# Column statistics from transposed messages, nodes in two parts, and an opening with its row tables shared out anew

## The reference, cut to what matters

```python
h = concatenate([x[dst], x[src], edge_attr], axis=1)            # x here is layernorm(x)
gate = sigmoid(_bn(silu(h @ W1f + b1f) @ W2f + b2f, g_int, beta_int))
msg = gate * (silu(h @ W1m + b1m) @ W2m + b2m)
agg = segment_sum(msg, dst, num_segments=N)
x = x + relu(xln + _bn(agg, g_bn, beta_bn))                     # _bn: mean and variance over the rows of each column
xn = layernorm(x)
gate_logits = xn @ Wg + bg + bias;  top-2 of 8, softmax -> combine
h = relu(einsum('td,edh->teh', xn, W1) + b1)
y = einsum('teh,ehd->ted', h, W2) + b2
x = x + einsum('ted,te->td', y, combine)
```

## Time and profile before

| | |
|---|---|
| median of three executions | 841.52 us |
| the profiled execution | 839.38 us |
| its span | 837.3 us |
| TensorE busy | 783.9 us (94%) |
| VectorE / ScalarE / GpSimd busy | 518.7 / 451.9 / 454.9 us |
| mean granted clock of TensorE | 0.965 of 2.4 GHz |

### The profile page before, as it was taken

One profiled execution on the slowest core, in us unless ns is written; L12 is line 12 of the kernel. 1 busy time (PEld: TensorE's weight loads), 2 busy tenths in 40 slices (PEclk: granted clock), 3 DMA queues, 4 the chain that ended last, 5 costly groups with the idle time before them and its releaser, 6 DMA issues. The chain is left out here.

```text
span 837.3 us, 14474 instructions
## 1 busy us (share of the span) xinstructions
PE 783.9 (94%) x4536; PEld 677.4 (81%) x4537; DVE 518.7 (62%) x885; ACT 451.9 (54%) x796; POOL 454.9 (54%) x390
## 2 busy tenths in 40 slices
PE   4789999999999999999999989999999963999998
PEld 3567888888888888888888878888888852999998
DVE  3357656565656666666565377778778846556564
ACT  2434454455454445555454477776766751747570
POOL 1477777777777777777776055554544553100000
PEclk9899999999999999999999989999999975899999
DMA  6889999999999999999999756665655612003101
GB/s 176 226 256 332 356 331 342 338 337 322 334 332 334 343 339 335 337 335 334 336 327 372 270 194 222 233 221 205 241 201 200 226 30 85 1 27 101 50 25 32
DMA packets 67754, 201.73 MB, mean 241 GB/s; under 512 B 10912, under 2 KB 18878, under 8 KB 67726
## 3 DMA queue, kind: packets, MB, share of 16 engines
q1 hardware_dynamic: 41614, 118.38, 40.2%
q0 software_dynamic: 25024, 81.94, 29.3%
q10 hardware_dynamic: 1088, 1.05, 0.5%
...
## 5 line engine op out<-in xcount | busy, mean ns | idle before, releaser
L122 POOL DMA_INDIRECT pre<-table_dst,idx x157 | 174.0, 1108 | 50.0 <-issue 47.5
L434 POOL DMA_INDIRECT from_src<-table_src,idx x157 | 154.7, 985 | 50.7 <-issue 46.9
L354 POOL TENSOR_TENSOR hvT_lo<-hv,hvT_hi 128x1024 fp32r<-128x1024 f32 x40 | 100.2, 2508 | 114.2 <-ACT hvT_hi L349 114.2
L565 PE MATMUL p_h<-eaT_hi,w_hi 128*128 128x512 f32 (+1 forms) x320 | 136.0, 425 | 1.5 <-DVE eaT_lo L490 1.5
L514 DVE TENSOR_TENSOR pre<-pre,from_src 128x512 f32<-128x512 f32 (+1 forms) x157 | 99.5, 694 | 49.0 <-DMA from_src<-table_src,idx 48.9
L565 PE MATMUL p_h<-eaT_lo,w_hi 128*128 128x512 f32 (+1 forms) x320 | 126.1, 394 | 0.0
L565 PE MATMUL p_h<-eaT_hi,w_lo 128*128 128x512 f32 (+1 forms) x320 | 125.2, 391 | 0.0
L528 DVE TENSOR_TENSOR h_lo<-h_full,h_hi 128x512 fp32r<-128x512 f32 (+1 forms) x80 | 54.4, 680 | 96.1 <-ACT h_full L469 96.0
L574 PEld LDWEIGHTS p_h<-ident,pre 128*128 128x128 f32 x628 | 77.4, 140 | 26.0 <-DVE pre L514 5.5
L574 PE MATMUL p_h<-ident,pre 128*128 128x128 f32 x628 | 94.2, 273 | 3.9 <-DVE pre L514 3.8
L468 ACT ACTIVATE h_hi<-p_h 128x512 fp32r<-128x512 f32 (+1 forms) x80 | 47.1, 588 | 91.4 <-PE p_h L574 91.4
...
## 6 DMA issues: line engine op xcount, KB each, us to landing
...
```

Of the source, the lines that this page charges most:

```text
L122: pool.indirect_dma_start(pre[b][0:n, t, :], None, table_dst, bass.IndirectOffsetOnAxis(ap=idx[b][0:n, t:t + 1], axis=0)).then_inc(got_dst ...
L354: nc.gpsimd.tensor_tensor(hvT_hl[b % 2][1][:], hv[b][:], hvT_hl[b % 2][0][:], ALU.subtract).then_inc(hv_lo, 1)
L434: pool.indirect_dma_start(from_src[b][0:n, t, :], None, table_src, bass.IndirectOffsetOnAxis(ap=idx[b][0:n, T + t:T + t + 1], axis=0)).the ...
L565: nc.tensor.matmul(p_h1[c][:, 0:w], w1_hl[wp][:, k, c * P:(c + 1) * P], eaT_hl[b % 2][dp][:, k, 0:w], start=n == 0, stop=False)
```

## The change

In the opening: ScalarE casts the source weights before the transposes of `x` and copies the destination rows, without bias, each behind a copy of `xT`; VectorE adds the bias to the source rows; the casts and splits of the edge weights move between them; SP stores the source rows before it loads the edge tile, and loads six column vectors instead of four (the scale and shift of the last batch norm are the new ones); GpSimd gathers the destination rows of group 0 as soon as the first index tile is ready. The first group's source gathers have a semaphore for each row tile, and VectorE's sum and TensorE's transposes go tile by tile there.

In the message block SP issues the five small loads that are left behind the experts' weights.

In the last block the sums over rows are replaced. TensorE transposes `agg` (ten transposes), VectorE takes batch-norm statistics along the rows of the transposed matrix and makes scale and shift on two columns; TensorE spreads these columns into rows by transposing a broadcast column, once for VectorE (read from PSUM) and once for ScalarE's copy, which GpSimd reads. Scaling, shifting and joining are separate operations: VectorE has tiles 0 to 2 without the shift of tile 2, GpSimd that and tiles 3 and 4. The row statistics, root, normalisation and low parts are done for tiles 0 to 2 and then for tiles 3 and 4. The first expert's first product starts with the left half of the nodes for all four pieces, when tiles 0 to 2 are split, and waits for the others before the right half.

```diff
...
-            load_ea(sp, 1, 1)
...
-            for n, v in enumerate((g_int, beta_int, b2f, b2m)):
+            load_ea(sp, 1, 1)
+            for n, v in enumerate((g_int, beta_int, b2f, b2m, g_bn, beta_bn)):
...
                 nc.gpsimd.tensor_copy(idx[b][:], idx_num[:, b, :]).then_inc(idx_ok, 1)
+                if b == 0:
+                    pool.wait_ge(idx_ok, 1)
+                    gather_dst(pool, 0)
...
-            gather_dst(pool, 0)
...
+            def src_weights_lo(k):
+                dve.wait_ge(wab_hi, 2)
+                nc.vector.tensor_tensor(w1ab_hl[1][:, 1, k], w1ab[:, 1, k], w1ab_hl[0][:, 1, k],
+                                        ALU.subtract).then_inc(wab_lo, 1)
...
-                dve.wait_ge(row_psum, t + 1)
-                nc.vector.tensor_tensor(rows[0][:, t, :], p_row[t % 4], b1_bc[:], ALU.add).then_inc(dst_ok, 1)
+                dve.wait_ge(row_psum, NT + t + 1)
+                nc.vector.tensor_tensor(rows[1][:, t, :], p_row[(NT + t) % 4], b1_bc[:],
+                                        ALU.add).then_inc(src_ok, 1)
...
             x_lo(NT - 1)
+            for k in range(KF):
+                src_weights_lo(k)
+            dve.wait_ge(w1_split, 1)
+            nc.vector.tensor_tensor(w1_hl[1][:], w1raw[:], w1_hl[0][:], ALU.subtract).then_inc(w1_split, 1)
...
                                     ALU.subtract).then_inc(w2_split, 1)
+            add_bias(2)
...
                                     ALU.subtract).then_inc(w2_split, 1)
+            for t in range(3, NT):
+                add_bias(t)
...
-            for t in range(NT):
+            act.wait_ge(wab_in[1], 32)
+            nc.scalar.copy(w1ab_hl[0][:, 1], w1ab[:, 1]).then_inc(wab_hi, 1)
+            def x_hi(t):
...
-            act.wait_ge(wab_in[1], 32)
-            nc.scalar.copy(w1ab_hl[0][:, 1], w1ab[:, 1]).then_inc(wab_hi, 1)
+            def dst_rows(t):
+                act.wait_ge(row_psum, t + 1)
+                nc.scalar.copy(rows[0][:, t, :], p_row[t % 4]).then_inc(dst_ok, 1)
+            x_hi(0)
+            x_hi(1)
+            for t in range(2, NT):
+                x_hi(t)
+                dst_rows(t - 2)
...
             nc.scalar.copy(w1_hl[0][:], w1raw[:]).then_inc(w1_split, 1)
+            for t in range(NT - 2, NT):
+                dst_rows(t)
+            act.wait_ge(ids_psum, 1)
+            nc.scalar.copy(idx_num[:, 0:NF, :].rearrange("p g c -> p c g"), p_ids).then_inc(ids_spread, 1)
...
-                        ap=idx[b][0:n, T + t:T + t + 1], axis=0)).then_inc(got_src[b], 16)
+                        ap=idx[b][0:n, T + t:T + t + 1], axis=0)).then_inc(
+                            got_first[t] if first and b == 0 else got_src[b], 16)
...
-            def sum_rows(i, b, short=False):
+            def sum_rows(i, b, short=False, first=False):
...
-                dve.wait_ge(got_src[b], 16 * T * i + 16 * len(rows))
+                if not first:
+                    dve.wait_ge(got_src[b], 16 * T * (i - (b == 0)) + 16 * len(rows))
                 for t, n in rows:
+                    if first:
+                        dve.wait_ge(got_first[t], 16)
...
-                    for c in range(C):
-                        add_rows(g, b, c, False)
+                    for t in range(T):
+                        pe.wait_ge(summed_ok, t + 1)
+                        for c in range(C):
+                            last = nc.tensor.matmul(p_h1[c][:, t * TE:(t + 1) * TE],
+                                                    pre[b][:, t, c * P:(c + 1) * P], ident[:],
+                                                    start=False, stop=t == T - 1, is_transpose=True)
+                            if t == T - 1:
+                                last.then_inc(h1_psum, 1)
...
                 load_expert(sp, b, b)
+            for n, v in enumerate((bg, bias)):
+                sp.dma_start(gate_b[:, n, :], spread(v, NE)).then_inc(n_in, 16)
+            sp.dma_start(wg_sb[:], Wg.rearrange("(k p) e -> p k e", p=P)).then_inc(n_in, 16)
+            sp.dma_start(b1_sb[:], b1.rearrange("e (m p) -> (e m) p", p=P)).then_inc(n_in, 16)
+            sp.dma_start(b2_sb[:], b2).then_inc(n_in, 16)
...
+    def parts(pieces, halves_first=False):
+        if halves_first:
+            return [(q * KH + m, m, lo, up) for q, (lo, up) in enumerate(HALF) for m in pieces]
+        return [(2 * m + q, m, lo, up) for m in pieces for q, (lo, up) in enumerate(HALF)]
...
-            pool.wait_ge(rs_ok, 1)
+            pool.wait_ge(st_copied, 1)
+            nc.gpsimd.tensor_tensor(xln[:, ND - 1, :], xln[:, ND - 1, :], st_rows[:, 1, :],
+                                    ALU.add).then_inc(pool_norm, 1)
...
+                n = 1 + 3 * (t - ND)
+                nc.gpsimd.tensor_tensor(dev[:, t, :], agg[:, t, :], st_rows[:, 0, :],
+                                        ALU.mult).then_inc(pool_norm, 1)
+                nc.gpsimd.tensor_tensor(xln[:, t, :], xln[:, t, :], st_rows[:, 1, :],
+                                        ALU.add).then_inc(pool_norm, 1)
+                pool.wait_ge(pool_norm, n + 2)
+                nc.gpsimd.tensor_tensor(dev[:, t, :], dev[:, t, :], xln[:, t, :],
+                                        ALU.add).then_inc(pool_norm, 1)
...
+            act.wait_ge(var_ok, 1)
+            nc.scalar.activation(bn_col[:, 1, :], bn_col[:, 0, :], ACT.Sqrt).then_inc(std3_ok, 1)
+            act.wait_ge(b1_psum, 1)
+            nc.scalar.copy(b1T[:], p_b1T).then_inc(b1T_ok, 1)
...
             nc.scalar.copy(xnT_hl[0][:, :, N:NPAD], xnT[:, :, N:NPAD]).then_inc(pad_ok, 1)
+            act.wait_ge(st_psum, 3)
+            nc.scalar.copy(st_rows[:].rearrange("p a f -> p (a f)"), p_st).then_inc(st_copied, 1)
+            for n, (lo, up) in enumerate(((0, ND), (ND, NT))):
+                act.wait_ge(eps_ok, n + 1)
+                nc.scalar.activation(ln_std[:, lo:up], ln_std[:, lo:up], ACT.Sqrt).then_inc(std4_ok, 1)
+                for t in range(lo, up):
+                    act.wait_ge(xnT_psum, t + 1)
+                    nc.scalar.copy(xnT_hl[0][:, :, t * TP:(t + 1) * TP], p_xnT[t]).then_inc(xnT_hi, 1)
...
-            for t in range(NT):
-                act.wait_ge(xnT_psum, t + 1)
-                nc.scalar.copy(xnT_hl[0][:, :, t * TP:(t + 1) * TP], p_xnT[t]).then_inc(xnT_hi, 1)
...
+                for n, m, lo, up in parts(pieces, start):
...
-            nc.vector.memset(ones[:], 1.0).then_inc(ones_ok, 1)
...
+            for k in range(KF):
+                dve.wait_ge(aggT_psum, k + 1)
+                nc.vector.bn_stats(bn_st[:, k, 0:6], p_aggT[k][0]).then_inc(bn_done, 1)
+            for k in range(KF):
+                dve.wait_ge(aggT_psum, 2 * KF)
+                nc.vector.bn_stats(bn_st[:, k, 6:12], p_aggT[k][1]).then_inc(bn_done, 1)
+            for k in range(KF):
+                dve.wait_ge(bn_done, KF + k + 1)
+                nc.vector.bn_aggr(bn_mv[:, k, :], bn_st[:, k, :]).then_inc(bn_done, 1)
+            dve.wait_ge(bn_done, 3 * KF)
+            nc.vector.tensor_scalar(bn_col[:, 0, :], bn_mv[:, :, 1], EPS, None, ALU.add).then_inc(var_ok, 1)
...
+            then(nc.vector.reciprocal(bn_col[:, 2, :], bn_col[:, 1, :]))
+            nc.vector.tensor_tensor(bn_col[:, 2, :], bn_col[:, 2, :], vecs[:, 4, :],
+                                    ALU.mult).then_inc(scale_ok, 1)
+            dve.wait_ge(scale_ok, 1)
+            then(nc.vector.tensor_tensor(bn_col[:, 3, :], bn_mv[:, :, 0], bn_col[:, 2, :], ALU.mult))
+            nc.vector.tensor_tensor(bn_col[:, 4, :], vecs[:, 5, :], bn_col[:, 3, :],
+                                    ALU.subtract).then_inc(shift_ok, 1)
+            def normalize_sum(t):
                 nc.vector.scalar_tensor_tensor(out=x_sb[:, t, :], in0=dev[:, t, :], scalar=0.0,
                                                in1=x_sb[:, t, :], op0=ALU.max, op1=ALU.add).then_inc(x1_ok, 1)
+            def ln_statistics(lo, up):
+                for t in range(lo, up):
+                    dve.wait_ge(x1_ok, t + 1)
+                    nc.vector.bn_stats(ln_stats[:, t, :], x_sb[:, t, :]).then_inc(ln_done, 1)
+                for t in range(lo, up):
+                    dve.wait_ge(ln_done, lo + t + 1)
+                    nc.vector.bn_aggr(ln_mv[:, t, :], ln_stats[:, t, :]).then_inc(ln_done, 1)
+                dve.wait_ge(ln_done, 2 * up)
+                nc.vector.tensor_scalar(ln_std[:, lo:up], ln_mv[:, lo:up, 1], EPS, None,
+                                        ALU.add).then_inc(eps_ok, 1)
+            def ln_apply(lo, up, half):
+                dve.wait_ge(std4_ok, half + 1)
+                then(nc.vector.reciprocal(ln_std[:, lo:up], ln_std[:, lo:up]))
+                for t in range(lo, up):
+                    nc.vector.tensor_scalar(xln[:, t, :], x_sb[:, t, :], ln_mv[:, t, 0:1], ln_std[:, t:t + 1],
+                                            ALU.subtract, ALU.mult).then_inc(xn_ok, 1)
+            def ln_lo(lo, up):
+                for t in range(lo, up):
```

(60 more changed lines are left out.)

194 lines of the change are left out of this document (49 added, 145 removed).

## The result

The kernel after takes 831.59 us (median of four executions, 831.21 to 832.02) beside 841.33 us for the kernel before on the same chip (four executions, 840.15 to 841.59): a ratio of 0.9885, 95% interval 0.9863 to 0.9906. The forecast was 831.4. The profiled execution took 832.02 us, its span is 829.9. In the profile the forecast of 829.3 was 2.7 us off.

The account below looks back on a forecast made before the run. TensorE was taken as the bound except from message sums to first expert product (28.55 us). Closing 9.4 plus opening 0.7 made 10.1 us, from 841.5 to 831.4 us; range 827.9 to 835.6.

Parts of the forecast that it names:

- The closing, −9.4: From the end of the message sums to the first expert product: new statistics and two-part order save 9.4 us.
- The price of 0.88 us for a pair of tiles: Closing's joins and sums: VectorE and GpSimd share SBUF reads, so one tile on each engine takes 0.88 us.
- (b): Rival in the closing: VectorE and GpSimd overlap freely without sharing; 828.8 us, chance 0.12.
- (c): Rival in the closing: GpSimd's slow tiles and slow spreads make the second half late; 834.3 us, chance 0.11.
- The halves: First expert product: starts behind tile 4's transposes, so the two-part order pays only by covering the split of tiles 3 and 4.
- First product and router: nothing: Behind the closing: same 48 matmuls after a half-clock stretch, GpSimd's sums and expert loads hidden, so no change.
- The opening, −0.7: Opening and early edge groups: earlier gathers shorten TensorE's stalls, a gain of 0.7 us, bounds −1.0 and +1.9.
- the source gathers start when the last source store lands, 36.5 to 37.4: Opening: source gathers start at 36.5 to 37.4 us instead of 38.12.
- the lead of 1.1 us for the gathers: Early edge groups: GpSimd's lead of 0.7 to 1.9 us, taken as 1.1, ends TensorE's next two stalls earlier.
- The block's end: Opening block: SP's longer queue ends it at 35.75 us instead of 35.06, moving TensorE's first transposes to 36.2.
- rival (a): Opening turns over: SP's longer queue ends the block, the moved edge tile takes bandwidth; 833.1 us, chance 0.14.
- rival (d): Expert part slower than before: clock stays low through both first products; 843 us at 100 slow matmuls, chance 0.03.

Follow-up runs that it names:

- f7: e2 with GpSimd's operations on tiles 3 and 4 held back until VectorE has done its three sums; 829.54 us, ratio 0.9875.
- f5: e2 with the first expert's first product in the old order of groups, waiting for all five tiles to be split; 833.69 us, ratio 0.9914.
- f6: e2 with the transposes of tiles 3 and 4 put behind the second of the four left groups; 828.86 us, ratio 0.9872.
- e1: Changed opening and edge block with the message and expert part of the kernel before; 842.35 us, ratio 1.0015.
- e3: Kernel after with the two new column vectors loaded behind the small loads, not in the opening; 834.53 us, ratio 0.9924.
- f11: Kernel after with TensorE's transposes of the first group's rows output by output again, VectorE still summing by tile; 834.70 us, ratio 0.9936.
- f9: Kernel after with the edge tile of group 1 loaded right behind the weights, not behind the source stores; 832.33 us, ratio 0.9900.
- e4: e3 with the other four column vectors also moved, into the edge block behind the first four groups' loads; 837.30 us, ratio 0.9955.
- g4: Kernel after with group 0's destination gathers held back until all four index tiles and the fourth source row tile are ready; 831.39 us, ratio 0.9903.
- e2: Old opening with the new closing, the two batch-norm columns loaded behind the small loads; 829.77 us, ratio 0.9886.
- g13: e2 with the edits of both f6 and f7; 829.65 us, ratio 0.9880.
- g3: e2 with only the first group's sums and transposes going tile by tile in the old opening; 831.74 us, ratio 0.9890.

## Why the prediction was right, and where it wasn't

The forecast of the median was 0.2 us off, and that closeness is partly luck. Of its two terms the first, −9.4, was right by its steps. The second, −0.7 for the opening, didn't come: the closing alone has the ratio of both halves together. A third, counted as nothing, was −1.5 in the profile. And the two profiles, in which all the steps are read, lie 7.4 us apart and not the 10.1 forecast: −9.28 and −1.54, but +2.98 up to the end of the message sums.

**The closing, −9.4: right.** Measured −9.28 in the profile of after, with 19.57 to 19.6 us in seven other kernels that have this closing unchanged. The steps hold too, counted from the end of the message sums (prediction / profile): scale in PSUM 5.4 / 5.4, joins done 9.1 / 9.2, three sums 11.7 / 11.8, three tiles normalised 14.8 / 14.7, tile 4 normalised 19.0 / 19.1, first matmul 19.3 / 19.6. The price of 0.88 us for a pair of tiles, read from the three rows, was the one that had to be chosen, and f7 shows by its absence that it is sharing: 0.36 alone, 0.89 beside GpSimd. The spreads ran at TensorE's pace, 0.42 a pair. With that rivals (b) and (c) are out.
What the 9.3 us are made of is tested only in part. The change moves the small loads forward, too, and no run does only that. In the kernel before the second column sum waited for them until 690.9, while the first squared tile was ready at 689.2:

```profile
688.80 1.74 ACT L959 ACTIVATE sq<-dev 125x256 f32<-125x256 f32 x5 [3.96 <-DVE dev L1036]
```

So an estimate from these rows is that some 1.7 us of the gain would have come from issuing the loads earlier in the old closing, and the rest from the column statistics and the two parts.
The Trainium skill (SBUF — State Buffer, Who interferes with whom) says that a VectorE instruction with two SBUF inputs contends with a GpSimd one that reads SBUF; f7 agrees, 1.08 against 2.67. The prediction left out what the same section adds: that copies, casts and tensor_scalar can use both port pairs and then contend as well. The 1.92 us against 1.06 of the normalisation in f7 fits that; no run here shows which mode it was in.

**The halves: sound.** The prediction had the first product wait for all transposes, and the halves pay only by hiding the splits of tiles 3 and 4. f5 puts that at 1.45 us of the start, and about 1 us more for a clock that rises later in the product. f6 shows that the left half was waiting for nothing but those transposes: with them behind its second group it starts 3.0 us earlier and keeps 2.2 of these in its profile.

**"First product and router: nothing": off by 1.5.** The first product is as before (9.2 us, half clock for 4.45). The second first-stage product behind the gate logits, which are 20 short matmuls, took 8.54 to 8.64 us in six kernels and 7.04 in eight, nothing in between: either a stretch at half clock lies in it or none. With the old closing it was there in both kernels, with the new one in four of twelve. That gave the kernel after another 1.5 us. Which one a kernel gets wasn't explained by any edit, and only one execution of each is profiled, so I count this as chance with better odds, not as an effect shown.

**The opening, −0.7: failed.** The step that failed is "the source gathers start when the last source store lands, 36.5 to 37.4": they started at 39.03 (38.59 in e1), and with that the lead of 1.1 us for the gathers was gone. The last store's issue ended at 32.62, near the 32.35 forecast; what was wrong is the landing, which took 6.4 us where I had 4.2 to 5. The start of the gathers less the end of that issue, in all profiles: 4.9 to 5.6 us in the seven kernels with the old opening, 6.2 to 6.4 in the four that have the changed one with only the one edge tile behind the stores (after, e1, e3, f11), 5.9 in f9, 7.0 in e4, at most 5.3 in g4. Three things run beside these stores in the new order. The destination gathers are 3.2 us earlier, at 26.83 where I had 28; holding them back took away at least 0.9 to 1.1 us (g4). The edge tile behind the stores accounts for 0.3 to 0.5 (f9), a second one for 0.6 more (e4). The two more vectors show no effect on it: 6.2 without them (e3), as in f11 with them.
The block's end was misread too, 35.75 forecast and 37.19 measured, but e3, e4 and f9 bring it forward without a gain.
That this moment decides is supported, not shown. Sorted by G, the kernels stand nearly sorted by Z, from 37.44 / 121.38 to 40.61 / 128.90, and e3 and e4, where TensorE starts earlier and the gathers don't, have the latest Z. GpSimd issues the gathers back to back, 1.25 us each, and the sums of the next groups wait for them. But the six profiles with one and the same old opening (before, e2, f5, f6, f7, g13) already range from 37.81 to 38.84 in G, 121.69 to 123.04 in Z and 682.99 to 685.04 in O. The profile of before has the lowest O of them, so up to 2 of the +2.98 us are scatter of single executions, and the 0.9 us between 38.12 and 39.03 is no wider than this scatter either. The landing times do separate, 4.9 to 5.6 against 6.2 to 6.4.
The other misread part is the gap ahead of the gate product: I had TensorE's 16 transposes end 1.15 us earlier and ScalarE served 0.1 earlier; the profile has 50.76 for ScalarE's first copy, 0.5 later than I put it, and the gate product at 53.64 instead of 53.36. f11 shows what the gap was worth: closed by 1 us, it came back as a longer wait one group later.
What the opening costs in all stays open within some 2 us either way. e1 alone says +1.3 with an interval from −0.8 to +3.3; after and e2 have equal ratios. That no gain is shown is as far as the runs go. So of rival (a) the missing gain came, but not by the block's end, and by the edge tile only in part; its price of 1.7 in all isn't settled.
The prediction's range is worded wrongly as well: by its own bounds both in the good corner give 841.5 − 13.3 = 828.2 and both in the bad one 841.5 − 5.9 = 835.6, so 827.9 to 835.6 takes both corners in and doesn't leave them out.

**The clock, rival (d): didn't come.** It rose as in the kernel before, 4.45 us after the first product began. The Trainium skill (TensorE: Matmul & The Clock Gate, Part 4) says that transposes don't count for the clock as matmuls do; the row of 685.97 to 705.55, 29 matmul records, all of them transposes, at a granted clock of 0.50, agrees, but TensorE is busy for only 6.89 of 19.58 us there, so idleness could do the same, and no run here separates the two. Half-clock stretches elsewhere go with part of the scatter: of e2's six executions the four at a mean granted clock of 0.971 took 829.53 to 829.85 us, the ones at 0.967 and 0.965 took 832.50 and 834.19. One place where profiles differ is near 480 us. Before the message block come the short matmuls of the last edge group. The table by stage of the kernel before there:

```profile
478.00:482.00 4.00, 2.85 (x23) 2.62 (x22) 0.35 (x3) 2.45 (x6) 1.33 (x1) 0.87 0.95 354
482.00:486.00 4.00, 2.88 (x7) 2.30 (x8) 3.37 (x4) 1.49 (x2) 4.00 (x3) 0.50 0.43 152
486.00:490.00 4.00, 3.49 (x14) 2.36 (x12) 3.06 (x11) 3.86 (x5) 0.05 (x1) 0.77 0.31 116
```

and of the kernel after:

```profile
478.00:482.00 4.00, 4.00 (x30) 3.72 (x28) 1.20 (x4) 1.35 (x6) 0.00 (x0) 0.90 0.95 305
482.00:486.00 4.00, 2.91 (x13) 2.74 (x14) 0.39 (x2) 2.37 (x6) 2.51 (x2) 0.50 0.62 252
486.00:490.00 4.00, 3.98 (x9) 3.13 (x10) 3.67 (x10) 2.61 (x4) 2.78 (x2) 0.50 0.54 196
490.00:494.00 4.00, 3.86 (x18) 2.82 (x17) 3.15 (x6) 3.77 (x6) 1.10 (x1) 0.82 0.18 72
```

Clock lost is (1 − granted) times length: 0.52 + 2.00 + 0.92 = 3.4 us before, 0.40 + 2.00 + 2.00 + 0.72 = 5.1 after. In eight of the fourteen profiles it is 3.4, in six 5.1, and nothing between: 3.4 in six of the seven with the old opening and in g4 and e3, 5.1 in g3 and in the other five with the changed one. Part of it lies where TensorE waits anyway.
